# Attention scores of two heads at a time in two 32-row groups of TensorE, read from the staged halves instead of from a stacked copy

## What is computed

```
q = heads(x @ Wq + bq); k = heads(x @ Wk + bk); v = heads(x @ Wv + bv)
scores = einsum('bhqd,bhkd->bhqk', q, k) * scale        # 256 x 256 for each head, over 32 features
scores = where(mask == 0, -inf, scores)
out = softmax(scores) @ v  ->  @ Wo + bo
```

## Time and profile before

| | |
|---|---|
| median of 3 runs | 1844.52 us (1842.23 to 1845.1) |
| the profiled execution's own time | 1843.87 us |
| its span in the profile | 1842.1 us |
| TensorE busy (matmul) | 96% of the span, 16817 matmuls |
| VectorE busy | 84% |
| ScalarE busy | 59% |
| GpSimd busy | 28% |
| mean granted TensorE clock | 0.991 |

### The profile page before, as it was taken

The page is one execution under the profiler, slowest core; times in us unless marked ns, Lnnn a source line. Parts: engine busy times, 40 slices in busy tenths (PEclk is TensorE's granted clock), DMA queues, the critical chain, the costliest instruction groups (busy, mean ns, idle before and its releaser), DMA issues.

```text
span 1842.1 us, 53154 instructions
## 1 busy us (share of the span) xinstructions
PE 1762.0 (96%) x16817; PEld 1410.2 (77%) x16817; DVE 1547.1 (84%) x4586; ACT 1094.3 (59%) x2445; POOL 511.3 (28%) x1286
## 2 busy tenths in 40 slices
PE   3889999999999999999999999999999999999996
PEld 2567878787888887787878788887778787877873
DVE  5778888888888888888888888888888888888883
ACT  2456665666656666666566666656666666666651
POOL 2023232233222233322223322323332222333111
PEclk9999999999999999999999999999999999999998
DMA  3422222322222232222232222223222222222220
GB/s 118 153 57 65 71 85 82 89 74 71 68 76 83 83 90 71 70 64 82 83 87 75 71 71 73 83 82 91 71 72 62 82 83 86 79 70 71 63 63 23
DMA packets 195401, 142.48 MB, mean 77 GB/s; under 512 B 36000, under 2 KB 167072, under 8 KB 195360
## 3 DMA queue, kind: packets, MB, share of 16 engines
q1 hardware_dynamic: 178224, 108.93, 20.8%
q10 hardware_dynamic: 17136, 33.03, 5.6%
HBM read 57.94 MB, written 16.78 MB: 41 GB/s over the span
## 4 chain that ended last, share of the span: by engine, by line
PE 81%; DVE 9%; issue 5%; ACT 2%; SPq 2%; DMA 1%; POOL 0%; ACTq 0%; DVEq 0%; POOLq 0%
PE ring L380 58%; PE turned L445 10%; PE score L430 5%; PE pv L463 3%; DVE val L920 2%; PE ring L498 2%; SPq L333 2%; DVE probs L828 2%; PE pv L465 1%; DVE work L888 1%; DVE probs_t_lo L836 1%; ACT val L657 1%; ACT stage L650 1%; PE ring L530 1%; DVE tops L761 0%
## 5 line engine op out<-in xcount | busy, mean ns | idle before, releaser
L619 ACT ACTIVATE probs_t_hi<-turned 128x512 f16<-128x512 f32 x512 | 305.2, 596 | 319.7 <-PE turned L445 318.7
L609 ACT ACTIVATE probs<-probs,least 128x256 f32<-128x256 f32 x1024 | 461.8, 505 | 6.7 <-DVE least L828 6.6
L828 DVE CUSTOM_DVE_ANT_0 probs<-score,far,undo_score 128x256 f32<-128x256 f32 x1024 | 449.7, 476 | 11.8 <-DVE far L1012 9.4
L1123 POOL TENSOR_TENSOR heads_out<-o_sum,o_rcp 128x64 f32<-128x64 f32 x512 | 146.9, 308 | 1043.3 <-DVE o_sum L849 1034.0
L836 DVE TENSOR_TENSOR probs_t_lo<-turned,probs_t_hi 128x512 f16<-128x512 f32 x512 | 349.4, 682 | 28.6 <-ACT probs_t_hi L619 24.9
L445 PE MATMUL turned<-ident,probs 128*128 128x128 f32 x2048 | 308.7, 273 | 6.2 <-ACT probs L609 6.1
L445 PEld LDWEIGHTS turned<-ident,probs 128*128 128x128 f32 x2048 | 246.5, 141 | 49.1 <-ACT probs L609 7.9
L430 PE MATMUL score<-stack 128*128 128x256 f16 x1024 | 196.2, 273 | 3.9 <-DMA stack<-stage 3.9
L463 PE MATMUL pv<-val,probs_t_hi 128*128 128x65 f16 x2048 | 184.4, 191 | 4.6 <-DVE probs_t_lo L836 4.2
L465 PE MATMUL pv<-val,probs_t_lo 128*128 128x33 f16 x2048 | 178.0, 179 | 0.0
L463 PEld LDWEIGHTS pv<-val,probs_t_hi 128*128 128x128 f16 x2048 | 157.5, 97 | 11.9 <-DVE probs_t_lo L836 6.0
(11 more groups left out here) (163 smaller groups left out, 4236.0 us busy)
## 6 DMA issues: line engine op xcount, KB each, us to landing
stack<-stage SPq DMA_DIRECT2D x2048, 32.0 KB, 1.9
xin<-x_dram ACTq DMA_DIRECT2D x32, 512.0 KB, 3.9
out_dram<-xo SPq DMA_DIRECT2D x32, 512.0 KB, 2.9
xa<-x_dram ACTq DMA_DIRECT2D x31, 512.0 KB, 3.7
adj_in<-adj_dram SPq DMA_DIRECT2D x32, 256.0 KB, 2.8
adjt_in<-adj_t_dram SPq DMA_DIRECT2D x32, 256.0 KB, 2.9
wq_raw<-wq_dram SPq DMA_DIRECT2D x2, 512.0 KB, 6.4
wk_raw<-wk_dram SPq DMA_DIRECT2D x2, 512.0 KB, 8.1
```

The source lines that it names most:

```text
L609: last = nc.scalar.activation(probs[:, u % 2, q, :], probs[:, u % 2, q, :], ACT.Exp, bias=least[:, u % 2, q:q + 1], scale=-1.0)
L619: nc.scalar.activation(pH[:, u % 2, :, :], turned[u % 2][:].rearrange("p (k n) -> p k n", k=QT), ACT.Copy).then_inc(hi["p"], 1)
L828: last = nc.vector.tensor_tensor_reduce(out=probs[:, u % 2, q, :], in0=score[u % 2][:, q * NODES:(q + 1) * NODES], in1=far[:, q, :], scale ...
L1123: last = nc.gpsimd.tensor_tensor(dst, o_sum[:, pair % 2, q:q + 3:2, :], o_rcp[:, pair % 2, q:q + 3:2].unsqueeze(2).broadcast_to([P, 2, HEAD]),
```

## The change

`scores` now does nothing for an odd head, and for an even head u computes the heads u and u + 1 together. It reads `stage` directly: the 32 partitions of a head as they stand there. For each half of the queries it issues the three products (high by high, high by low, low by high) in turn, each for head u and then for head u + 1, accumulating in the two banks `score[0]` and `score[1]`: 12 matmuls of 32 rows and 256 columns. The fourth product (low by low) is no longer computed. It waits for the low halves of the group on VectorE, and for `masked` of head u - 1, since both banks must be free; one semaphore increase of 2 at the last matmul reports both heads. The tile `stack`, its eight semaphores, `stack_heads` and its DMAs are gone. Everything else is unchanged.

```diff
-            def stack_heads(g, b):
-
-                par = g % 2
-                sp.wait_ge(lo["qk"], count(b, 4, g))
-                for i in range(GROUP):
-                    for j in range(4):
-                        first, second = j // 2, 2 + j % 2
-                        sp.dma_start(
-                            stack[HEAD * j:HEAD * (j + 1), par, i, :, :],
-                            stage[HEAD * i:HEAD * (i + 1), par, first:second + 1:second - first, :]
-                            ).then_inc(stacked[par][i], 16)
...
             def scores(u, b):
 
-                g, i = u // GROUP, u % GROUP
-                pe.wait_ge(stacked[g % 2][i], count(b, 2, g // 2) * (16 * 4))
+                if u % 2:
+                    return
+                g, pair = u // GROUP, (u, u + 1)
+                pe.wait_ge(lo["qk"], count(b, 4, g))
                 if u >= 2:
-                    pe.wait_ge(masked, count(b, HEADS, u - 2))
+                    pe.wait_ge(masked, count(b, HEADS, u - 1))
                 elif started(b - 1):
-                    pe.wait_ge(masked, count(b - 1, HEADS, HEADS + u - 2))
+                    pe.wait_ge(masked, count(b - 1, HEADS, HEADS - 1))
                 for q in range(QT):
-                    last = nc.tensor.matmul(score[u % 2][:, q * NODES:(q + 1) * NODES],
-                                            stack[:, g % 2, i, 0, q * P:(q + 1) * P],
-                                            stack[:, g % 2, i, 1, :], start=True, stop=True)
-                last.then_inc(mm["score"], 1)
+                    for s, (of_q, of_k) in enumerate(((0, 2), (0, 3), (1, 2))):
+                        for v in pair:
+                            rows = slice(HEAD * (v % GROUP), HEAD * (v % GROUP + 1))
+                            last = nc.tensor.matmul(score[v % 2][:, q * NODES:(q + 1) * NODES],
+                                                    stage[rows, g % 2, of_q, q * P:(q + 1) * P],
+                                                    stage[rows, g % 2, of_k, :],
+                                                    start=(s == 0), stop=(s == 2))
+                last.then_inc(mm["score"], 2)
```

More of the change, by code:

```diff
@@ L178, in two_layers @@
         stage = sb("stage", [P, 2, 4, NODES], f16)
-        stack = sb("stack", [P, 2, GROUP, 2, NODES], f16)
         val = sb("val", [P, QT, HEADS, VPITCH], f16)
@@ L219, in two_layers @@
         adj_got, adjt_got = sem("adj_got"), sem("adjt_got")
-        stacked = [[sem(f"stacked{par}{i}") for i in range(GROUP)] for par in range(2)]
         stored = sem("stored")
@@ L349, in body @@
                     load_late(1)
-                if cur:
-                    stack_heads(2, t)
                 if cur and not prev:
@@ L355, in body @@
                     store(p - 1)
[L356 to L360, removed]
             def store(b):
```

## The result

| | before | with the change |
|---|---|---|
| median | 1844.08 us (1842.23 to 1845.1, 4 runs) | 1941.26 us (1939.15 to 1942.78, 4 runs) |
| span in the profile | 1842.1 us | 1938.3 us |
| ratio | | 1.0527, 95% interval 1.0509 to 1.0546 |

The change makes the kernel 97 us slower. The forecast was 1953 us, within a range of 1902 to 2105.

The account below looks back on a forecast made before the run. The prediction took TensorE, busy 54.54 of 55 us in a steady stretch, as the bound. From 1843.9 us it added 56 (matmuls), 42 (changes of rows) and 29 (added wait), less 15 (waits) and 3 (DMAs): 1953 us, range 1902 to 2105.

Parts of the forecast that it names:

- What bounds it: TensorE's stream has no holes in the steady part, so whatever it is given on top comes out at the end.
- Matmuls of a pair: Scores on TensorE: two heads' matmuls stream at once, a pair takes 0.65 us in place of 0.435; +56 us.
- The serial rival: Scores on TensorE: row groups do not overlap, +223 us in place of +56, 2078 to 2212 us; chance 0.20.
- Going to 32 rows and back: TensorE, around each pair's scores: 512 changes of rows at 82 ns each, half the 164 ns latency; +42 us.
- The reading of the Trainium skill's drain: Changes of rows on TensorE: changing tiling mode drains it, the full 164 ns each; 84 us, sum 1995.
- The wait that is added: Step 12: scores wait 0.95 us for VectorE's mask(13) in 31 graphs; +29 us, bounds 20 to 35.
- steps 0 and 2 would just hold: No mask wait ahead of the scores there: 0.08 us left in step 0, 0.04 in step 2.
- Waits that go: TensorE's two waits for `val`, 7.9 and 6.7 us, should close as head 7 comes earlier and even steps lengthen; -15 us.
- The DMAs that go: Stack DMAs: their only wait is 3.9 us at the start, nothing in the steady part; -3 us.
- Blocked weight loads: A row group's weights can't load while it computes: 2.2 us for a pair, +457, 2312 us; chance 0.05.
- the rule that the prediction gives beside this rival: Trainium skill: weight loads overlap with matmuls in flight only when the row group differs; 2312 us by it.
- The faster one: Scores on TensorE: matmuls feeding a quarter of the rows take less than 0.109 us; time 1828 us; chance 0.02.

Follow-up runs that it names:

- same_group: The changed kernel with both heads of a pair read from the even head's rows, so all 12 matmuls are in one row group: 2108.52 us, 1.1435 of before.
- mask_first: The changed kernel with mask(13) of step 11 moved ahead of the second layer's softmax pieces and turned_low(11) on VectorE: 1922.01 us, 1.0437 of before.
- best_early_loads: `stack_pairs_mask_first` with graph 0's eight late weight loads issued ahead of its stack DMAs instead of among them: 1827.49 us, 0.9906 of before.
- stack_pairs_mask_first: The kernel before, stack and 128-row matmuls kept, with the change's pair order and waits, and mask(13) moved as in `mask_first`: 1834.16 us, 0.9955 of before.
- six_and_six: The changed kernel with all six products of head u written first, then all six of head u + 1: 1997.43 us in one run.
- head_by_head: The changed kernel with, for each half of the queries, three products of head u written before the three of head u + 1: 1944.77 us, 1.0546 of before.

## Why the prediction held, point by point

- **What bounds it.** Right. TensorE's stream had no room, and what was put on it came out at the end: `same_group` was forecast at 2107 and measured 2108.5.
- **Matmuls of a pair, +56.** Right in kind and size: 55.8. The two heads stream at once, and `same_group` shows that it takes different row groups. The serial rival would have had starts of 0.109 us in the twelve. The 0.65 us that the prediction named from the first start to the last but one is that of six distances; there are five, 0.56 us.
- **Going to 32 rows and back, +42.** Right in kind, sized too low: 54.3, by 0.212 us for a pair in place of 0.164. The reading of the Trainium skill's drain with the whole latency gave 84 and was too high. The cost was unknown from the trace of before, and half of the latency was a guess that fell near: luck, not a reading.
- **The wait that is added, +29.** Its place was right, at 26 in all, but only 0.66 of the 0.83 us are the wait for mask(13) that the prediction described, 20 us; `mask_first` took that part away. VectorE's chain took 3.27 us from turn(11) in place of 3.33, and part of the wait covers the 0.1 us that the way into the 32-row matmuls costs in any case. The other 0.17 us the prediction had not seen: step 11 has lost 0.22 us, so TensorE comes to turn(12) before ScalarE has its exponentials. The weight loads of `turned` now wait for them 40 times, 14.1 us in all, in place of 8 times and 7.9. It was right, too, that steps 0 and 2 would just hold: both have the plain 205 ns ahead of the first score.
- **Waits that go, -15.** The direction was right and the size half of what came: -32. This is the largest miss of the sum. I took the 7.9 and 6.7 us from the idle column of the earlier trace rows. But idle time is counted from the modelled end of the last matmul, which lies behind the point at which the next could have started. Before, step 6 of the graph of the earlier trace rows shows:

```profile
899.67 0.18 PE L465 MATMUL pv<-val,probs_t_lo 128*128 128x33 f16 x1
900.12 1.24 PE L498 MATMUL ring<-ident,xa 128*128 128x128 f32 x8 [0.27 <-DVE val L920]
```

  The idle time is 0.27 us, but the starts are 0.44 us apart, where 26 ns is the pace: 0.42 lost. Another 0.33 us of the step was lost in four distances of 0.16 to 0.23 us in place of 0.11, which no idle time shows at all. In step 0 the starts at the same wait were 0.37 us apart.
- **The DMAs that go, -3.** Nothing in the steady part, as said. The wait of 3.9 us is gone, and graph 0 as a whole lost 6.8, of which the DMAs are shown for that wait alone. `best_early_loads` shows that the stack's DMAs there stood behind the loads of the weights: with the loads moved, the wait for them is gone from TensorE's list (4.3 us in `stack_pairs_mask_first`), and graph 0 is 5.5 us shorter.
- **The rivals.** Serial groups are out by the starts 3 to 5 ns apart. Blocked weight loads are out by `same_group`: each matmul there has its own weight load, all in one row group, and they start 109 ns apart; so the rule that the prediction gives beside this rival doesn't hold here for 32 rows either. The faster one is out by the couples' 109 ns.
- **The sum.** It came within 12 us partly by luck: the changes of rows cost 12 us more than their term, and the added wait, the stalls and what graph 0 gave back came out 3, 17 and 5 us below theirs, so that the errors partly cancel.

## What to carry to other kernels

Where TensorE is full, count the distances of its starts. A matmul of 32 rows took as long here as one of 128 (0.109 us from start to start), so small ones pay only if enough row groups stream together. Here two groups, with three products for each head, took 0.65 us for a pair. The stack put all of it into 0.435, and its DMAs cost nothing in the steady part. Only two of the four row groups are in use; whether four heads at once would stream at the same pace (0.65 us against the stack's 0.87, an estimate from the couples) no run here shows. Count 0.2 us of TensorE for each way from 128 rows into 32 and back, and put as many small matmuls as can be into one visit. And when a stall on TensorE is to be priced, take the distance of starts less the plain pace; the idle column leaves out the part of a stall that the latency of the last matmul covers, and shows nothing of a stall shorter than that.

## What had not been expected of the hardware

TensorE starts matmuls out of their written order when their row group is free and that of the earlier ones is not: it passed three in `six_and_six` (and two in `head_by_head`), so a hand-made interleaving gained next to nothing over runs of three (a graph takes 57.52 us in place of 57.57). So the sentence ahead of the prediction, that each engine executes its own list in its written order, doesn't hold for the starts of TensorE's matmuls in different row groups. And a 32-row matmul that follows in its own row group has its weights loaded beside the one before, at the plain 109 ns.
